# A Strassen-style block product in place of an ordinary one, inside a fused two-layer adapter kernel

## The chip, the core and the metric

The kernel runs on one core of one Trainium2 chip. The metric is the device time of one execution in microseconds, the median of three runs. TensorE (PE) does the matrix products and 128x128 transposes, with weight loads (PEld) that overlap it. VectorE (DVE), ScalarE (ACT) and GpSimd (POOL) work element by element, and SyncE (SP) issues most transfers. The engines run their own programs in order and meet only at semaphores.

## What is computed

The input x is 8 batches of 256 rows by 1024. Two layers are applied, each of which adds to x the result of two adapted linear maps with gates. Cut to the second layer, which the change is about:

```python
base_out = jnp.einsum('bti,oi->bto', x, W) + b          # cond map, 1024x1024
lora_out = jnp.einsum('btr,bro->bto', jnp.einsum('bti,bir->btr', x, A), Bm)   # adapter of the batch
y = base_out + lora_out * SCALING
base = y @ W_base.T + b_base                            # ffn map, 1024x1024
logits = y @ W_router.T                                 # 8 experts, the top 2 are kept
lora = jnp.einsum('ter,te,eor->to', jnp.einsum('td,erd->ter', y, A1), w, B1) * SCALING
x = x + base + lora
```

## The kernel before

Since nothing nonlinear stands between the two maps, the kernel folds them once: M = W · [router, A1, W_base]ᵀ, plus the identity for the residual, is a matrix of 1024 rows (8 tiles of 128) and 1160 columns; 16 more columns hold the adapter A of the batch, so 1176 in all. Each float32 number is split into a high and a low part of the type fp32r, and each product of two split numbers is three matmuls (`three`, L1054 to L1056: hi·hi, hi·lo, lo·hi). The helper `lo` (L705) makes a low part on VectorE, ScalarE copies the high part.

The stages are these. First the weights come in and are turned, and the first layer's small matrices are made (`turn_units`, L1049). Then the **fold** goes over 8 rows of M: each row is 24 steps of `three` in three parts of 392, 512 and 256 columns (`m_chunk`), into one of two sets of three PSUM banks. Beside it VectorE multiplies the bias into `b_acc` (`b_times`, L934), which is written out at the end by six matmuls with `ones`.

Then come eight **slots**, one for each batch, of which the first seven also prepare the next batch. Slots 1 to 4 are a hardware loop. In slot b, TensorE does the **main product** of x1 (the batch after the first layer, turned, hence 8 tiles by 2 halves of 128 rows) with M: 48 steps of `three`, six groups (2 halves by 3 parts of 392 columns) of 8 steps, into the banks `pm`. Among these steps stand, at places written out by hand (`main_to(n)` goes on to step n):

- `small0`: the first layer's 272 columns for one half of the next batch (24 matmuls, L1054 with `C0hi`), twice;
- turns of small gate matrices (`hg`, `wh`, `wz`, L1103, and `hs`, L1244), which VectorE's gate computations `gates0`, `gates1` and `top1` must have made;
- `lora`: for each half 4 matmuls for each of 3 parts (240, 392 and 392 columns), which add the expert part to y;
- `ffn0` in four groups of 6 matmuls of 256 columns: the next batch's first-layer result, which VectorE adds to x (`x1_add`, L871). The groups go to three banks, so that only the fourth waits for an `x1_add`:

```python
                if has_a:
                    pe.wait_ge(whT_lo, a + 2)
                    for g in range(3):
                        ffn0(q, g, X1W_BANKS[g])
                main_to(34)
                turn_hs(m + 1)
                if has_a:
                    pe.wait_ge(x1_sum, q * 4 + 1)
                    ffn0(q, 3, X1W_BANKS[3])
```

The output rows are copied from PSUM to `ybuf` by ScalarE (L572) and stored. GpSimd does nothing in the slots.

## Time and profile before

| what | value |
| --- | --- |
| median of 3 runs | 500.59 us (500.29 to 501.21) |
| the profiled execution | 501.62 us, its span 499.6 us |
| TensorE busy | 487.5 us (98%), 3007 matmuls |
| VectorE, ScalarE, GpSimd busy | 267.6, 135.9 and 9.5 us |
| granted clock of TensorE, mean | 0.989 of 2.4 GHz |

The span goes from the first to the last instruction; about 2 us of the time lie outside it. TensorE is busy almost throughout, and a record of a matmul lasts longer than its share of the array, since matmuls are pipelined: what a matmul costs in a stream is the distance from its start to the next one's start.

### The profile page before, as it was taken

Reading aid. Unit: us, or ns where it says so; the run is one execution under the profiler, and the core shown is the slowest. Engines: PE = TensorE matmul, PEld = TensorE weight load, DVE = VectorE, ACT = ScalarE, POOL = GpSimd, SP = SyncE. Lnnn points to the kernel's source line nnn. Section 1 sums busy time; section 2 is a strip of 40 time slices with the busy share of each in tenths; the row PEclk is TensorE's granted clock in tenths of the full one; section 3 lists DMA queues with packets and bytes.
Section 4 is the critical chain, followed back from the end, with each engine's and each line's share of the span. In section 5 each row is a group of like instructions: output and inputs, shape, how many; then the busy total and the mean of one; then the engine's idle time right before and its main releaser. Section 6 shows DMA issues by size and latency. Waiting matters only on the chain.

```text
span 499.6 us, 8465 instructions
## 1 busy us (share of the span) xinstructions
PE 487.5 (98%) x3007; PEld 466.5 (93%) x3007; DVE 267.6 (54%) x825; ACT 135.9 (27%) x300; POOL 9.5 (2%) x18
## 2 busy tenths in 40 slices
PE   6999999999999988999999999999999999999997
PEld 4988899999999878999999999999999999999997
DVE  3745864544446746475465574656557457445211
ACT  4444630111111331232132232132124123212111
POOL 2040000000000000000000000000000000000000
PEclk9987999999999999999999999999999999999999
DMA  8975525221111145107304312611710910200111
GB/s 258 331 253 178 183 72 139 106 63 43 42 42 48 44 62 78 54 4 120 71 5 95 53 46 64 83 42 60 89 42 2 148 44 2 64 31 16 59 42 43
DMA packets 86621, 40.22 MB, mean 81 GB/s; under 512 B 68503, under 2 KB 80545, under 8 KB 86462
## 3 DMA queue, kind: packets, MB, share of 16 engines
q1 hardware_dynamic: 86318, 39.25, 31.3%
q0 software_dynamic: 272, 0.56, 0.5%
q8 instruction: 19, 0.31, 0.3%
q14 instruction: 12, 0.10, 0.1%
HBM read 28.64 MB, written 11.16 MB: 80 GB/s over the span
## 4 chain that ended last, share of the span: by engine, by line
PE 96%; DVE 2%; DMA 1%; ACT 1%; issue 0%; DVEq 0%; ACTq 0%
PE banks L1054 28%; PE banks L1056 28%; PE banks L1055 28%; PE banks L1049 5%; PE banks L1068 3%; PE banks L1239 2%; PE banks L1103 1%; DMA a0f<-in_L_ffn_A_dram 1%; PE banks L1077 0%; PE banks L1201 0%; PE banks L1244 0%; DVE xTlo L705 0%; DVE x_raw L752 0%; PE banks L1249 0%; DVE a0f L741 0%
## 5 line engine op out<-in xcount | busy, mean ns | idle before, releaser
L1054 PE MATMUL banks<-Mhi,x1Thi 128*128 128x392 f32 x384 | 137.0, 357 | 2.0 <-DVE x1Tlo L705 1.5
L1055 PE MATMUL banks<-Mlo,x1Thi 128*128 128x392 f32 x384 | 130.6, 340 | 0.0
L1056 PE MATMUL banks<-Mhi,x1Tlo 128*128 128x392 f32 x384 | 130.5, 340 | 0.0
L1054 PEld LDWEIGHTS banks<-Mhi,x1Thi 128*128 128x128 f32 x384 | 72.3, 188 | 4.5 <-issue 2.4
L1054 PE MATMUL banks<-WbThi,ws_hi 128*128 128x392 f32 (+2 forms) x216 | 74.7, 346 | 0.0
L1056 PE MATMUL banks<-WbThi,ws_lo 128*128 128x392 f32 (+2 forms) x216 | 73.2, 339 | 0.0
L1055 PE MATMUL banks<-WbTlo,ws_hi 128*128 128x392 f32 (+2 forms) x216 | 73.0, 338 | 0.0
L1055 PEld LDWEIGHTS banks<-Mlo,x1Thi 128*128 128x128 f32 x384 | 72.5, 189 | 0.0
L1056 PEld LDWEIGHTS banks<-Mhi,x1Tlo 128*128 128x128 f32 x384 | 72.2, 188 | 0.0
L1056 PEld LDWEIGHTS banks<-WbThi,ws_lo 128*128 128x128 f32 x216 | 40.7, 188 | 3.2
L1055 PEld LDWEIGHTS banks<-WbTlo,ws_hi 128*128 128x128 f32 x216 | 40.6, 188 | 3.1
L1054 PEld LDWEIGHTS banks<-WbThi,ws_hi 128*128 128x128 f32 x216 | 40.6, 188 | 3.0
L572 ACT ACTIVATE ybuf<-banks 128x392 f32<-128x392 f32 (+1 forms) x48 | 21.8, 454 | 44.3 <-PE banks L1239 44.3
L1054 PE MATMUL banks<-C0hi,xThi 128*128 128x272 f32 x112 | 32.5, 290 | 1.3 <-DVE xTlo L705 1.3
L624 ACT ACTIVATE Mhi<-banks 128x392 f32 (+5 forms) x24 | 10.3, 494 | 81.3 <-DVE banks L951 60.9
L1056 PE MATMUL banks<-C0hi,xTlo 128*128 128x272 f32 x112 | 32.3, 288 | 0.0
L1055 PE MATMUL banks<-C0lo,xThi 128*128 128x272 f32 x112 | 32.2, 287 | 0.0
L503 ACT ACTIVATE x1Thi<-wraw 128x512 fp32r<-128x512 f32 x32 | 19.8, 627 | 21.4 <-DVE wraw L871 19.1
L705 DVE SCALAR_TENSOR_TENSOR Mlo<-banks,Mhi 128x392 f32 (+8 forms) x30 | 15.4, 554 | 16.4 <-ACT Mhi L624 14.4
L1054 PEld LDWEIGHTS banks<-C0hi,xThi 128*128 128x128 f32 x112 | 21.1, 188 | 1.8 <-DVE xTlo L705 1.8
L705 DVE SCALAR_TENSOR_TENSOR x1Tlo<-wraw,x1Thi 128x512 fp32r<-128x512 f32 x32 | 21.1, 682 | 2.2 <-ACT x1Thi L503 2.2
L705 DVE SCALAR_TENSOR_TENSOR xTlo<-x_raw,xThi 128x512 fp32r<-128x512 f32 x28 | 18.1, 688 | 6.9 <-ACT xThi L503 6.9
(180 smaller groups left out, 772.8 us busy)
## 6 DMA issues: line engine op xcount, KB each, us to landing
wraw<-in_L_cond_W_dram SPq DMA_DIRECT2D x16, 512.0 KB, 3.9
out_dram<-ybuf SPq DMA_DIRECT2D x15, 512.0 KB, 3.1
x_raw<-in_x_dram SPq DMA_DIRECT2D x56, 128.0 KB, 3.9
wraw<-in_L_ffn_W_base_dram SPq DMA_DIRECT2D x8, 512.0 KB, 6.5
xin_first<-in_x_dram SPq DMA_DIRECT2D x1, 1024.0 KB, 9.5
x1T_dram<-xin_first SPq DMA_DIRECT2D x1, 1024.0 KB, 3.9
wraw<-x1T_dram SPq DMA_DIRECT2D x2, 512.0 KB, 3.5
Fbuf<-fe_hi_dram SPq DMA_DIRECT2D x16, 64.0 KB
```

Source lines behind the costliest of these rows:

```text
L503: act.activation(dst, src, ACT.Copy).then_inc(ready, 1)
L572: act.activation(ybuf[:, y0:y0 + n], pm[c][:, PART - n:PART], ACT.Copy).then_inc(y_ready, 1)
L624: act.activation(Mhi[:, bass.ds(i * 2 + par, 1), R + c0:R + c0 + n], m_psum(M_BANKS[par], c).unsqueeze(1), ACT.Copy).then_inc(m_hi, 1)
L705: return dve.scalar_tensor_tensor(out=out_, in0=src, scalar=scale, in1=hi.bitcast(F32), op0=ALU.mult, op1=ALU.subtract)
L1049: ins = pe.transpose(unit_bank(q)[:, col:col + width], src, ident[0:kp, 0:kp])
L1054: pe.matmul(out_, l[0], r[0], start=start, stop=False, **kw)
L1055: pe.matmul(out_, l[0], r[1], start=False, stop=False, **kw)
L1056: return pe.matmul(out_, l[1], r[0], start=False, stop=stop, **kw)
L1068: ins = pe.matmul(banks[:, k, 0:2 * RC], w, R0T[:, j, :], start=j == 0 and n == 0, stop=j == K - 1 and n == 1)
L1103: pe.transpose(dst, src, ident[:, :]).then_inc(done, 1)
L1239: pe.matmul(y, hsT[:, :], Fbuf[:, s], start=False, stop=True, skip_group_check=True)\
```

## The change

The main product becomes two parts. 256 of the 1176 columns (16 of the adapter, 136 of router and A1, 104 of y) stay an ordinary product, `zd`: 16 steps of `three`, 256 wide. The other 920 columns are taken as two halves of 460, the 8 tiles of the inner dimension as two groups of 4, and the two row halves as the third split. This 2x2x2 block product is done with seven products (`PRODUCTS`) instead of eight, each of 4 steps of `three` of 460 columns, 28 steps. A slot has 44 steps in place of 48.

The right-hand factors B11, B21, B22 and T1 to T4 are made during the fold (sums of blocks of M, then split into high and low), whose row order becomes 0, 4, 1, 5, ... and whose parts become 240, 460 and 460 columns. The left-hand ones are the blocks A11 to A22 of x1 and the sums S1 to S4, made in place in `x_raw`. GpSimd makes the sums (`s_sums`), the low parts of S3 and S4 (`s_lo_part`) and the low parts of the next x tiles (`xT_lo_part`), which VectorE made before. The products are combined in `ybuf` by six VectorE additions beside copies by ScalarE. The banks are short: all four `ffn0` groups now share the bank `x1w`. The low parts of x1 for a batch are all made before its slot (`a_part`).

```diff
-    MW = MC + R
     ZC = R + RC
-    HALF = D // 2
-
-    PART = MW // 3
-    Y_OF = [(0, PART - ZC), (PART - ZC, PART), (2 * PART - ZC, PART)]
+
+    DW = 256
+    SW = (R + MC - DW) // 2
+    KH = K // 2
+    Y_OF = [(0, DW - ZC), (DW - ZC, SW), (DW - ZC + SW, SW)]
+    CHUNKS = [(0, DW - R), (DW - R, SW), (DW - R + SW, SW)]
     LANG_BIAS = 5.0
...
+            def s_sums(q, turn):
+                raw = x_raw[turn]
+                gp.wait_ge(a_lo, q * 4 + 4)
+                gp.tensor_tensor(raw_block(raw, 1, 1), raw_block(raw, 1, 0), raw_block(raw, 1, 1), ALU.add)\
+                  .then_inc(s_raw, 1)
+                gp.wait_ge(s_raw, q * 4 + 1)
+                sub(raw_block(raw, 1, 0), raw_block(raw, 0, 0), raw_block(raw, 1, 0)).then_inc(s_raw, 1)
+                gp.wait_ge(s12_lo, q * 2 + 1)
+                sub(raw_block(raw, 1, 1), raw_block(raw, 1, 1), raw_block(raw, 0, 0)).then_inc(s_raw, 1)
+                gp.wait_ge(s_raw, q * 4 + 3)
+                sub(raw_block(raw, 0, 1), raw_block(raw, 0, 1), raw_block(raw, 1, 1)).then_inc(s_raw, 1)
+
+            def s_lo_part(q, turn, n):
+                left = left_of(turn)[("S3", "S4")[n]]
+                gp.wait_ge(s_hi, q * 4 + 3 + n)
+                sub(left[:, 1, :], raw_block(x_raw[turn], 1 - n, n), left[:, 0, :].bitcast(F32)).then_inc(s34_lo, 1)
+
+            gp.wait_ge(x_turned, 1)
...
+            def b_times(k):
+
+                for n in range(2):
+                    for c, (c0, w) in enumerate(CHUNKS):
+                        nth = 2 * k + n
+                        dve.wait_ge(acc_step, 3 * nth + c - 1 if nth else 1)
+                        dve.scalar_tensor_tensor(out=b_acc[:, c0:c0 + w], in0=Wb_of[c][n][:, k, :].bitcast(F32),
+                                                 scalar=bcol[:, k:k + 1], in1=b_acc[:, c0:c0 + w],
+                                                 op0=ALU.mult, op1=ALU.add).then_inc(acc_step, 1)
...
+                par, row, p = s % 2, M_ROWS[s], s // 2
+                add_ident(s)
+                dve.wait_ge(w1_hi, s + 3)
+                lo(ws_lo[par][:, :], wraw[2 + par][:, :], ws_hi[par][:, :]).then_inc(w1_lo, 1)
+                dve.wait_ge(m_hi, m_hi_at(s, 1))
+                lo(direct(1, row), m_psum(par, 0), direct(0, row)).then_inc(m_lo, 1)
+                if p < 2 and par == 0:
+                    dve.wait_ge(m_hi, m_hi_at(s, 2))
+                    lo_right(p, B11, m_psum(par, 1), m_lo)
+                    dve.wait_ge(m_hi, m_hi_at(s, 3))
+                    sub(right_raw(p, T1), right_raw(p, T3), m_psum(par, 1), m_lo)
+                elif p < 2:
+                    dve.wait_ge(m_hi, m_hi_at(s, 3))
+                    sub(right_raw(p, T3), m_psum(par, 2), right_raw(p, T3), m_lo)
+                    sub(right_raw(p, T2), m_psum(par, 2), right_raw(p, T1), m_lo)
+                    lo_right(p, B21, m_psum(par, 1))
+                    lo_right(p, B22, m_psum(par, 2))
...
+                for k in ((s,), (4, 5), (6, 7))[max(0, s - 3)]:
+                    b_times(k)
+            dve.wait_ge(x2_in, 128)
+            for half in range(2):
+                turn_x(half, x_raw[1])
+
+            for s in (LAST, K - 1):
+                dve.wait_ge(m_hi, m_hi_at(s, 1))
+                lo(direct(1, M_ROWS[s]), m_psum(s % 2, 0), direct(0, M_ROWS[s])).then_inc(m_lo, 1)
...
+                s_part(b, turn, 1)
                 if has_a:
                     gates0(a, q)
+                hs_part(m, 0)
+                if has_a:
                     hgT_part(a)
-                hs_part(m)
+                hs_part(m + 1, 1)
                 if has_a:
                     top1(a)
-                    if first:
-                        turn_x(1, x_raw[1], x_in[1], 64)
-                        xT_turned(a + 1, 1, x_raw[1])
-                    gates1(m, lambda: whT_part(a, 0))
-                    gates0(a + 1, q, lambda: wzT_part(m))
-                    if has_n:
-                        turn_x(0, x_raw[turn], x_in[0], b * 64 + 64)
+                gates1(m, 0, (lambda: whT_part(a, 0)) if has_a else None)
+                gates1(m + 1, 1, None)
+                wzT_part(m)
+                if has_a:
+                    gates0(a + 1, q)
+                keep_p16(b)
+                if has_a:
                     hgT_part(a + 1)
+                if has_n:
+                    dve.wait_ge(x_in[0], b * 64 + 64)
+                    turn_x(0, x_raw[turn])
+                keep_p15(b)
+                if has_a:
                     top1(a + 1)
+                wzT_part(m + 1)
+                if has_a:
                     whT_part(a + 1, 1)
-                    if has_n:
-                        xT_turned(n, 0, x_raw[turn])
-                    add(0)
-                    hs_part(m + 1)
-                    add(1)
-                    split(0)
-                    add(2)
-                    gates1(m + 1, lambda: add(3))
-                    split(1)
-                    wzT_part(m + 1)
-                    split(2)
-                    split(3)
-                else:
-                    gates1(m, None)
-                    wzT_part(m)
-                    hs_part(m + 1)
-                    gates1(m + 1, None)
-                    wzT_part(m + 1)
                 if has_n:
-                    turn_x(1, x_raw[turn], x_in[1], b * 64 + 128)
-                    xT_turned(n + 1, 1, x_raw[turn])
+                    dve.wait_ge(x_in[1], b * 64 + 64)
+                    turn_x(1, x_raw[turn])
+                if has_a:
+                    x1_add(q, 0, raw)
+                    x1_add(q, 1, raw)
+                    x1_add(q, 2, raw)
+                    a_part(q, 1 - turn, 0)
+                keep_p167(b)
+                if has_a:
+                    x1_add(q, 3, raw)
+                    a_part(q, 1 - turn, 1)
+                    a_part(q, 1 - turn, 2)
+                    a_part(q, 1 - turn, 3)
+                y_c21(b)
+                y_c22(b)
                 if has_a:
                     as_part(q)
-            slot(0, 0, True, True, first=True)
+                    s_part(q, 1 - turn, 0)
+                y_c12(b)
...
             turn_units(NU2, units_b1)
-            pe.wait_ge(w1_lo, K)
-            pe.wait_ge(m_lo, 3 * (K - 2))
-            m_chunk(K // 2 - 1, 1, 0)
+            pe.wait_ge(m_kept, 2)
+            m_chunk(0, 1)
+            pe.wait_ge(acc_step, 1 + 6 * K)
+            pe.wait_ge(gp_step, 3)
+            pe.wait_ge(m_lo, m_lo_at(K - 1, 1))
+
+            def bias_part(c):
+                c0, n, _ = BIAS_PARTS[c]
+                pe.matmul(bias_psum(c), ones[:, :], b_acc[:, c0:c0 + n], start=True, stop=True).then_inc(bias_done, 1)
+
+            bias_part(0)
+            bias_part(1)
+            pe.wait_ge(m_kept, 4)
+            m_chunk(1, 1)
+            pe.wait_ge(brow_lo, 1)
+            bias_part(2)
+            m_chunk(0, 2)
+            m_chunk(1, 2)
...
+                PRODUCTS = [("A11", B11, ca, True), ("S2", T2, cb, True), ("A22", T4, ce, True), ("S1", T1, cd, True),
+                            ("A12", B21, ca, False), ("S3", T3, cb, False), ("S4", B22, cd, False)]
...
                     turn_small(wh_ready, a + 2, pt_wh, wh[:, :], twh_done)
-                main_to(31)
+                main_to(38)
                 if has_a:
                     pe.wait_ge(whT_lo, a + 2)
-                    for g in range(3):
-                        ffn0(q, g, X1W_BANKS[g])
-                main_to(34)
-                turn_hs(m + 1)
-                if has_a:
-                    pe.wait_ge(x1_sum, q * 4 + 1)
-                    ffn0(q, 3, X1W_BANKS[3])
-                main_to(35)
-                adapter(m + 1)
-                main_to(44 if has_n else 46)
-                turn_small(wz_ready, m + 2, pt_wz, wz[:, :], twz_done)
-                main_to(47 if has_n else 48)
-                pe.wait_ge(wzT_lo, m + 2)
-                lora(m + 1, 0)
-                lora(m + 1, 1)
-                main_to(48)
-                lora(m + 1, 2)
+                    pe.wait_ge(y_act, b * 3 + 1)
+                    for g in range(4):
+                        if g:
+                            pe.wait_ge(x1_sum, q * 4 + g)
+                        ffn0(q, g, x1w)
+                        main_to(39 + g)
+                main_to(42)
+                lora(m + 1, 1, 0)
+                lora(m + 1, 1, 1)
+                main_to(43)
+                pe.wait_ge(c_kept, b * 3 + 3)
+                lora(m + 1, 1, 2)
+                main_to(44)
```

The order of instructions shows three places. The first is TensorE in slot 0, between two groups of `ffn0` for the next batch (`whThi,BwThi` is the first matmul of three). Before:

```order
L1054 MATMUL banks<-whThi,BwThi 128x256
L1055 MATMUL banks<-whTlo,BwThi 128x256
L1056 MATMUL banks<-whThi,BwTlo 128x256
L1054 MATMUL banks<-whThi,BwThi 128x256
L1055 MATMUL banks<-whTlo,BwThi 128x256
L1056 MATMUL banks<-whThi,BwTlo 128x256
```

After the change, the same place (`G,left` is a step of a Strassen product, 460 wide):

```order
L1350 MATMUL banks<-whThi,BwThi 128x256
L1351 MATMUL banks<-whTlo,BwThi 128x256
L1352 MATMUL banks<-whThi,BwTlo 128x256
L1350 MATMUL banks<-G,left 128x460
L1351 MATMUL banks<-G,left 128x460
L1352 MATMUL banks<-G,left 128x460
L1350 MATMUL banks<-whThi,BwThi 128x256 [waits x1_sum]
L1351 MATMUL banks<-whTlo,BwThi 128x256
L1352 MATMUL banks<-whThi,BwTlo 128x256
```

Between two groups stands one product step now, and the next group has a wait for `x1_sum`, the addition of the group ahead of it.

The second is VectorE from the end of slot 0 over the branch into the loop. Before:

```order
L705 SCALAR_TENSOR_TENSOR wzTlo<-banks,wzThi 128x128 [waits wzT_hi]
L705 SCALAR_TENSOR_TENSOR x1Tlo<-wraw,x1Thi 128x512 [waits x1T_hi] x2
L752 STREAM_TRANSPOSE x_raw<-x_raw 128x1024 [waits x_in1]
L705 SCALAR_TENSOR_TENSOR xTlo<-x_raw,xThi 128x4x128 [waits xT_hi] x2
L705 SCALAR_TENSOR_TENSOR Mlo<-asraw,Mhi 128x8x16 [waits as_hi]
L1031 UNCONDITIONAL_BRANCH
L1031 ISA
L779 ISA [waits p0_done]
```

After, where `left<-x_raw,left` is the low part of S1 in the first row and of S2 in the fifth:

```order
L909 SCALAR_TENSOR_TENSOR left<-x_raw,left 128x512 [waits s_hi]
L1084 TENSOR_TENSOR ybuf<-banks,ybuf 128x460 [waits p_done]
L1327 UNCONDITIONAL_BRANCH
L1327 ISA
L909 SCALAR_TENSOR_TENSOR left<-x_raw,left 128x512 [waits s_hi]
L977 ISA
L978 ISA [waits p0_done]
L978 TENSOR_TENSOR lgc<-banks,bias 128x8
```

The gates of the new slot (`lgc`, which waits for `p0_done`) now stand behind the low part of S2 and no more right behind the adapter's split.

The third is GpSimd's program at the end of the fold. Before, its last instructions:

```order
L481 TENSOR_TENSOR C0lo<-a0f,C0hi 128x4x136 [waits c0_hi]
L481 TENSOR_TENSOR C0lo<-b_j,C0hi 128x4x136 [waits c0_hi]
L484 DMA a0c<-in_L_ffn_A_dram 128x1024 [waits unit_done]
L485 DMA routers<-in_L_ffn_W_router_dram 8x1024
L488 COPY b_j<-b0raw 128x1024 [waits b1_in,c0_lo]
L490 MEMSET Fbuf 96x1024 [waits m_done]
```

After, `x_raw<-x_raw` are the four sums of `s_sums(0, 0)`:

```order
L596 TENSOR_TENSOR x_raw<-x_raw 128x512 [waits a_lo]
L586 TENSOR_TENSOR x_raw<-x_raw 128x512 [waits s_raw]
L586 TENSOR_TENSOR x_raw<-x_raw 128x512 [waits s12_lo]
L586 TENSOR_TENSOR x_raw<-x_raw 128x512 [waits s_raw]
L586 TENSOR_TENSOR xTlo<-x_raw,xThi 128x512 [waits xT_hi] x2
L586 TENSOR_TENSOR left<-x_raw,left 128x512 [waits s_hi] x2
```

The third sum, the one for S2, waits for `s12_lo`, the low part of S1 on VectorE, since it overwrites S1.

## Rows read from the trace of the kernel before

**Rows 1.** The page, busy time of each engine and the chain that ended last.

```profile
PE 487.5 (98%) x3007; PEld 466.5 (93%) x3007; DVE 267.6 (54%) x825; ACT 135.9 (27%) x300; POOL 9.5 (2%) x18
...
PE 96%; DVE 2%; DMA 1%; ACT 1%; issue 0%; DVEq 0%; ACTq 0%
```

**Rows 2.** The chain of waits, TensorE alone: waited for, us in total, times, longest.

```profile
PE banks L1054 <- DVE x1Tlo L705: 1.5, 1, 1.5
PE banks L1054 <- DVE xTlo L705: 1.3, 1, 1.3
```

**Rows 3.** Windows, one steady slot and the last slot.

```profile
231.54:271.63 40.09, 40.09 (x258) 39.73 (x257) 23.06 (x87) 10.71 (x27) 0.00 (x0) 1.00 0.36 62
466.10:499.60 33.50, 30.48 (x174) 29.76 (x174) 5.28 (x30) 4.52 (x13) 0.00 (x0) 0.98 0.15 54
```

**Rows 4.** Timeline of TensorE from a slot's start: start us, us, instruction.

```profile
224.82 0.29 PE L1054 MATMUL banks<-C0hi,xThi 128*128 128x272 f32 x1
...
227.81 0.34 PE L1054 MATMUL banks<-Mhi,x1Thi 128*128 128x392 f32 x1
...
231.54 0.27 PE L1103 MATMUL banks<-ident,hg 128*128 128x128 f32 x1
```

**Rows 5.** Timeline of TensorE: 240 columns, and 136 columns.

```profile
29.32 0.28 PE L1056 MATMUL banks<-R0T,b0lo 128*128 128x136 f32 x1
29.43 0.28 PE L1054 MATMUL banks<-R0T,b0hi 128*128 128x136 f32 x1
...
302.58 0.27 PE L1054 MATMUL banks<-ws_hi,wzThi 128*128 128x240 f32 x1
...
303.03 0.34 PE L1054 MATMUL banks<-ws_hi,wzThi 128*128 128x392 f32 x1
```

**Rows 6.** Timeline of TensorE: the parts of one fold row, and what follows.

```profile
152.54 0.34 PE L1054 MATMUL banks<-WbThi,ws_hi 128*128 128x392 f32 x1
...
156.84 0.39 PE L1054 MATMUL banks<-WbThi,ws_hi 128*128 128x512 f32 x1
...
162.41 0.28 PE L1054 MATMUL banks<-WbThi,ws_hi 128*128 128x256 f32 x1
...
165.24 0.27 PE L1049 MATMUL banks<-ident,wraw 128*128 128x128 f32 x1
```

**Rows 7.** Groups by line and form: busy us, mean ns, idle before.

```profile
L871 DVE TENSOR_TENSOR wraw<-banks,x_raw 128x512 f32<-128x512 f32 x28 | 19.2, 687 | 1.2 <-PE banks L1056 1.1
L705 DVE SCALAR_TENSOR_TENSOR x1Tlo<-wraw,x1Thi 128x512 fp32r<-128x512 f32 x32 | 21.1, 682 | 2.2 <-ACT x1Thi L503 2.2
L705 DVE SCALAR_TENSOR_TENSOR Mlo<-banks,Mhi 128x392 f32 x6 | 3.4, 567 | 8.9 <-ACT Mhi L624 8.9
L934 DVE SCALAR_TENSOR_TENSOR b_acc<-WbTlo,bcol,b_acc 128x1160 f32<-128x1160 f32 x8 | 11.4, 1427 | 0.9
L752 DVE STREAM_TRANSPOSE x_raw<-x_raw 128x1024 f32<-128x1024 f32 x14 | 17.3, 1236 | 0.0
L503 ACT ACTIVATE x1Thi<-wraw 128x512 fp32r<-128x512 f32 x32 | 19.8, 627 | 21.4 <-DVE wraw L871 19.1 <-PE banks L1056 2.2
L481 POOL TENSOR_TENSOR C0lo<-a0f,C0hi 128x544 fp32r<-128x544 f32 x1 | 1.4, 1353 | 0.4 <-ACT C0hi L525 0.4
```

**Rows 8.** Timeline of all engines: the gates of a slot, and the turned gate.

```profile
228.13 0.17 DVE L779 TENSOR_TENSOR lgc<-banks,bias 128x8 f32<-128x8 f32 x1 [0.76 <-PE banks L1056]
...
230.20 0.29 DVE L774 TENSOR_TENSOR hg<-banks,gc 128x128 f32<-128x128 f32 x1
...
231.91 0.28 ACT L503 ACTIVATE hgThi<-banks 128x128 fp32r<-128x128 f32 x1 [3.01 <-PE banks L1103]
232.22 0.29 DVE L705 SCALAR_TENSOR_TENSOR hgTlo<-banks,hgThi 128x128 fp32r<-128x128 f32 x1 [1.73 <-ACT hgThi L503]
```

**Rows 9.** Timeline: TensorE goes on after a wait for VectorE.

```profile
222.82 0.38 PE L1054 MATMUL banks<-ws_hi,wzThi 128*128 128x240 f32 x1 [0.21 <-DVE wzTlo L705]
223.03 0.28 PE L1055 MATMUL banks<-ws_lo,wzThi 128*128 128x240 f32 x1
```

More of the change, by code:

```diff
@@ L493, in _ @@
+            slot(0, 0, True, True)
+            with gp.Fori(0, 2) as i:
+                for turn in (1, 0):
+                    slot(i * 2 + 2 - turn, turn, True, True)
+            slot(NB - 3, 1, True, True)
+            slot(NB - 2, 0, True, False)
+            slot(NB - 1, 1, False, False)
         @block.scalar
@@ L650, in _ @@
-            keep_m(K // 2 - 1, 1, (2,))
-            def slot(b, turn, has_a, has_n, first=False):
+                    a_part(0, 0, 0)
+                act.wait_ge(bias_done, c + 1)
+                keep(b_acc[0:64, c0:c0 + n].bitcast(F32R), bias_psum(c)[0:64, :], brow_hi)
+            act.wait_ge(m_done, m_count(K - 1, 1))
+            for which, i in ((B11, 0), (B21, 2), (B22, 3)):
+                keep(right(2, which)[0], m_raw[:, i, :], g2_hi)
+            act.wait_ge(m_ident, LAST + 1)
+            keep(right(3, B11)[0], m_psum(0, 1), g3_hi)
@@ L865, in x1_first, with x1_add @@
                    .then_inc(x1_sum, 1)
[L867 removed]
+            def x1_add(q, g, raw):
                 dve.wait_ge(x1w_done, q * 4 + g + 1)
[L870 to L875 removed]
@@ new lines, in main_to @@
+                def main_to(until):
+                    for step in range(done[0], until):
+                        if step < 2 * K:
+                            half, k = step // K, step % K
+                            name = ("A11", "A12", "A21", "A22")[step // KH]
+                            if step == 0:
+                                pe.wait_ge(a_lo, b * 4 + (2 if first else 3))
+                                if first:
+                                    pe.wait_ge(m_lo, m_lo_at(K - 1, 1))
+                            if step == K:
+                                wait_earlier(pe, y_act, b * 3 if not first else 0)
+                                pe.wait_ge(a_lo, b * 4 + 4)
+                                if first:
+                                    pe.wait_ge(g3_lo, 2)
+                            ins = three(zd[half][:, :], (rows(left[name][:, 0, :], k % KH), rows(left[name][:, 1, :], k % KH)),
+                                        (Mdir[:, 0, k, :], Mdir[:, 1, k, :]), k == 0, k == K - 1, skip_group_check=True)
+                            if k == K - 1:
+                                ins.then_inc(h1_done, 1)
+                        else:
+                            i, k = steps[step - 2 * K]
+                            name, which, bank, fresh = PRODUCTS[i]
+                            if k == 0:
+                                before(i)
+                            if first and step == 2 * K:
+                                pe.wait_ge(g_lo, 8)
+                                pe.wait_ge(g2_lo, 7)
+                            if first and k == KH - 1:
+                                pe.wait_ge(g3_lo, 7 if i else 1)
+                            ins = three(bank, (rows(left[name][:, 0, :], k), rows(left[name][:, 1, :], k)),
+                                        right(k, which), fresh and k == 0, k == KH - 1, skip_group_check=True)
+                            if k == KH - 1:
+                                ins.then_inc(p_done, 1)
```

775 lines of the change are left out of this document (479 added, 296 removed).

## The prediction

> **What bounds the kernel now.** First the page: TensorE is busy for 487.5 of the span's 499.6 us, it has 96% of the chain that ended last, and VectorE, at 267.6, has 2% of it [rows 1]. So what counts is the length of TensorE's stream and its holes. Then TensorE's waits: inside the work only two are over 1 us, 1.5 and 1.3, both for low parts by VectorE at the passage from the fold to slot 0 [rows 2]. Then the windows: a steady slot is 40.1 us without a hole, at clock 1.00; VectorE is busy for 23.1 of it, ScalarE for 10.7, GpSimd not at all. The last slot is 33.5, 30.5 of it TensorE [rows 3]. Last the timeline, for what a matmul costs from start to start (start times below are differences of its rows). 21 matmuls of 392 columns take 3.73 us, .178 each, and 24 of 272 take 2.99, .125 [rows 4]. A fold row of 24 each of 392, 512 and 256 takes 4.30, 5.57 and 2.83: .179, .232 and .118 [rows 6]. The cost isn't in proportion to the columns: four of 240 take .45, .1125 each, and one of 136 takes .11 as well [rows 5]. Below 240 columns nothing more is saved. For 460 I lay a line between 392 and 512: .178 + 68/120 x .053 = **.208**.
>
> **The change part by part.** The sum is made against the profiled execution, 501.62.
>
> *Main product.* Before, 144 matmuls at .178 = 25.6 us in a slot. After, 16 x 3 at .118 and 28 x 3 at .208 = 5.7 + 17.5 = 23.1. 8 batches by 2.5: **-20.0**. If .208 is wrong by .005, this moves by 3.4.
>
> *Adapter output (`lora`).* Its parts go from 240, 392, 392 to 104, 460, 460. A set of one each: .1125 + 2 x .178 = .47, and .11 + .416 = .53. Four matmuls of each part, two halves, eight batches: 64 x .057 = **+3.7**. If a 104-wide matmul cost in proportion (.05) it would be 0; the 136-wide row is the nearest, so I take the floor.
>
> *Fold parts.* 24 x (.1125 + .416) = 12.7, as before (12.70): **0**.
>
> *The one bank of `ffn0`.* A group may start only when `x1_add` has emptied the bank. Group: 6 x .118 = .71, of which the last record ends .16 after the next could start (.28 against .118) [rows 6], so .87. The hop to VectorE .1 (ScalarE starts on the turned gate at 231.91, .1 after the record that began at 231.54 ended [rows 4, 8]); `x1_add` .69 [rows 7]; hop back .1; and the stream takes .1 more to fill (.21 instead of .11 after a wait [rows 9]). That is 1.8 us from group to group. In it lie the group and one step of a product, .71 + 3 x .208 = 1.33. The hole is .45, three times in seven slots: **+9.5**. Here VectorE has nothing else in its way, since the first three additions follow each other; the fourth has a low part and a copy ahead of it, which I take to fit in. Lower bound: if the end of the record is not what VectorE waits for, .2 to .3 a hole, 4 to 6 in all.
>
> *Slot 0.* Behind the fold's last matmul VectorE has the identity .3, ten operations of 460 columns at .6 (blocks of M, from the 392-wide .57), the low part of S1 .68: 7.3. GpSimd's third sum waits for that one: 1353 ns for 544 columns [rows 7] is 1.27 for 512, so 8.6. ScalarE .63, low part of S2 .68: 9.95. Behind it stand the gates, 2.35 from `lgc` to the end of `hg` (228.13 to 230.49) [rows 8]: 12.3. TensorE is at the turn of `hg` after 24 matmuls of the adapter, 3.0, and 12 steps of 3 x .118, at 7.3. It waits **+5.0**; `small0` and the product would be its cover, and both stand ahead. Bounds: 3, if half the VectorE operations lie before the fold's end, and 7.
>
> *End of the fold.* From the end of the sixth row VectorE has identity, `ws_lo` and a direct block, 3.3; the bias sweeps of two rows, four of them, 1.43 each as one piece [rows 7] and some 1.65 cut in three: 10.0; two transposes of 1.24: 12.5; two direct low parts: 13.2. TensorE has two 240-wide parts, a turn and one 460-wide part ahead of the bias matmuls, 2 x 2.7 + .8 + 5.0 = 11.2. **+2.0** (0 to 4). It is queued behind `acc_step` and the last `m_lo` alike.
>
> *Small terms.* The turning stage, where some units are split: **+.5** (0 to 2). The waits of [rows 2] go, since the blocks of A are ready before the slot: **-2.8**. The tail has two 460-wide additions at .63 one after the other instead of one copy: **+.3**.
>
> *In the steady slots*, the chain of S sums decides whether the gates hold TensorE up. From the slot's start: last low part of A at -1.0; first sum .35; high part 1.05, low part 1.75; third sum 3.05; high 3.75, low part of S2 4.45; gates 6.85. TensorE needs `hg` at 7.3. The slack is .4, so nothing is added. The other gate turns have .15 to .6 by the same count. VectorE's load goes from 23 to about 25.5 of 39, ScalarE's to about 12.5, GpSimd's from 0 to ten operations, 12.7. These are far from full. Slots of about 39.4.
>
> Sum: -20.0 + 3.7 + 9.5 + 5.0 + 2.0 + .5 - 2.8 + .3 = **-1.8**. So 499.8 against 501.62; the median of before is 500.59, 1.0 lower, and so is the forecast: **498.8**.
>
> **The rivals.**
>
> *The holes are half of what I walked.* A walk by mean durations adds each hop in full. If the ring costs .2 (-5), slot 0 and the fold's end 3.5 in place of 7 (-3.5) and `lora` nothing for its narrow part (-3.5 at most), the sum is about -12: **488.6**. For it: the kernel before shows hardly any wait but in [rows 2], with queues as long. Against: 136 columns at the price of 240 [rows 5], and a bank that is one instead of three. Chance .30.
>
> *GpSimd and VectorE hold each other up.* All ten GpSimd operations of a slot read two SBUF operands, while VectorE makes low parts of S and A from two SBUF operands too, and parts of the gates. No row of before has both at once: GpSimd's 1353 ns operation ran beside VectorE work with at most one SBUF operand, and the slots had no GpSimd work. If an operation of the one waits for the end of the other, each meeting costs up to 1.27 on VectorE's side or .68 on GpSimd's. The chain of S has two or three such places and a slack of .4, so 1.5 to 2.5 us of each of six slots would be lost, and 2 more in slot 0: +11 to +17, **about 511**. It decides from .5 us a slot on. For it: 12.7 us of GpSimd beside 25.5 of VectorE in 39. Against: no row. Chance .24. This is the case in which the kernel is slower.
>
> The Trainium skill, page "SBUF — State Buffer", section "Who interferes with whom", says that a VectorE instruction with two SBUF inputs contends with a GpSimd instruction that reads SBUF, and that the second then waits until the first has ended. By that rule this rival is the forecast; no trace here shows it so far.
>
> *A GpSimd sum takes longer than its only row*, by half, or the chain has more hops: 1.5 us late against a slack of .4 to .5 gives +1.0 in seven slots: **505.5**. Chance .12.
>
> **How the numbers follow.** The forecast as walked, within 3 us: .34, of which .19 lie on the faster side, .08 within and .07 on the slower. ±.2%, 1 us, is about what a measurement of this kernel can tell from no change. The half-size holes: .30 faster. The two slower rivals: .36, of which .02 within. That is .49 faster, .10 same, .41 slower. The predicted time is the forecast's, 498.8, which also lies between the cases; its own range is 495.5 to 502. The range for 8 in 10 reaches to both sides: 487 (the small holes, with 1.5 of room) to 511 (the lock).
>
> **What would show it.** Right: 460-wide matmuls .208 apart, 104-wide ones .11; waits for `x1_sum` of .4 to .5, three in a slot; one of about 5 us at the first turn of `hg` in slot 0 and of about 2 ahead of the bias matmuls; steady slots of 39.4 without a wait for gates; the last slot's TensorE time down from 30.5 to about 28.5 (-2.5 + .5). Wrong: GpSimd operations over 1.4 us or VectorE's low parts over .75 whenever both run (the lock); the `x1_sum` waits at .2 (the small holes); or waits for `hg`, `wz` or S high parts in every slot, which would say that my slack of .4 was none.

## The result: 526.5 us in place of 500.8, five per cent slower

The changed kernel takes 526.47 us (median of 4 runs, 525.70 to 527.38), the kernel before 500.80 on the same chip: a ratio of 1.049 (1.045 to 1.054). The forecast was 498.8, with a range up to 511. One execution of the kernel before, of 2687 us, counts as slow and is in none of the ratios below.

The page of the changed kernel, busy time of each engine and the chain that ended last, beside [rows 1]:

```profile
PE 483.9 (92%) x2911; PEld 438.3 (84%) x2911; DVE 341.3 (65%) x923; ACT 154.1 (29%) x339; POOL 112.0 (21%) x98
...
PE 48%; issue 24%; DVE 13%; POOL 8%; ACT 3%; DMA 2%; SPq 0%; POOLq 0%; DVEq 0%; ACTq 0%
```

TensorE has less work than before, and it isn't the bound any more: VectorE and GpSimd together have 21% of the chain. VectorE's busy time grew by 74 us. The forecast gave it 2.5 us more a slot; a good part of the rest isn't work but operations that last longer, as is seen below.

TensorE's waits (waited for, us in total, times, longest), beside [rows 2]:

```profile
PE banks L1399 <- DVE hg L973: 23.0, 7, 7.5
...
PE banks L1350 <- DVE x_raw L1069: 2.2, 14, 0.2
```

`hg` is the gated adapter tile of the next batch's first half. It is waited for once in each of the seven slots that prepare a batch. The second row is the one bank of `ffn0`.

Windows by stage, slot 0, slots 1 to 5, slot 6 and the last one. First the kernel before (length, then busy time of PE, PEld, DVE, ACT and POOL, clock, DMA share, GB/s):

```profile
184.15:224.82 40.67, 39.17 (x249) 38.16 (x248) 25.09 (x91) 10.41 (x27) 0.00 (x0) 1.00 0.35 54
224.82:425.37 200.55, 200.55 (x1282) 198.82 (x1281) 115.46 (x437) 54.18 (x137) 0.00 (x0) 1.00 0.32 60
425.37:465.60 40.23, 40.23 (x257) 39.61 (x256) 19.38 (x83) 9.25 (x25) 0.00 (x0) 1.00 0.11 34
465.60:499.60 34.00, 30.54 (x175) 29.80 (x174) 5.57 (x31) 4.99 (x14) 0.00 (x0) 0.98 0.15 53
```

The same stages of the changed kernel:

```profile
183.05:232.68 49.63, 41.65 (x244) 38.02 (x245) 34.93 (x102) 14.92 (x36) 14.50 (x12) 0.90 0.20 28
232.68:447.76 215.08, 199.78 (x1221) 181.62 (x1220) 151.49 (x456) 58.41 (x145) 63.87 (x51) 0.98 0.31 56
447.76:490.35 42.59, 39.26 (x246) 35.29 (x244) 26.59 (x91) 10.64 (x28) 10.71 (x10) 1.00 0.11 33
490.35:523.90 33.55, 28.37 (x162) 25.74 (x162) 12.16 (x39) 5.51 (x14) 6.33 (x5) 0.96 0.18 69
```

The differences: up to slot 0 -1.1 us, slot 0 +9.0, slots 1 to 5 +14.5, slot 6 +2.4, the last slot -.5. Together 24.3, the whole growth of the span (499.6 to 523.9). So the loss is not in the fold but in every slot that has gates for a next batch.

What ends late is seen in slot 2 of the changed kernel. VectorE from the low part of S1 to `hg` (start us, us, instruction, idle before it and what ended that):

```profile
275.75 1.22 DVE L909 SCALAR_TENSOR_TENSOR left<-x_raw,left 128x512 fp32r<-128x512 f32 x1 [0.54 <-ACT left L656]
...
279.03 1.23 DVE L909 SCALAR_TENSOR_TENSOR left<-x_raw,left 128x512 fp32r<-128x512 f32 x1 [1.51 <-ACT left L656]
280.18 0.15 DVE L978 TENSOR_TENSOR lgc<-banks,bias 128x8 f32<-128x8 f32 x1
...
281.51 1.33 DVE L1003 TENSOR_SCALAR gac<-iota,ixfc,wc 128x8 f32<-128x8 f32 x1
282.76 1.30 DVE L1006 TENSOR_SCALAR gbc<-iota,ixfc,wc 128x8 f32<-128x8 f32 x1
284.10 0.17 DVE L1009 TENSOR_TENSOR gc<-gac,gbc 128x8 f32<-128x8 f32 x1
284.63 0.29 DVE L973 TENSOR_TENSOR hg<-banks,gc 128x128 f32<-128x128 f32 x1 [0.37 <-DVE gc L1009]
```

And GpSimd in the same stretch:

```profile
275.13 1.29 POOL L586 TENSOR_TENSOR x_raw<-x_raw 128x512 f32<-128x512 f32 x1
277.05 2.66 POOL L586 TENSOR_TENSOR x_raw<-x_raw 128x512 f32<-128x512 f32 x2 [0.63 <-DVE left L909]
281.54 2.50 POOL L586 TENSOR_TENSOR xTlo<-x_raw,xThi 128x512 fp32r<-128x512 f32 x2 [1.83 <-ACT xThi L656]
```

Lay the two beside each other. The low part of S1 starts at 275.75, while GpSimd's sum runs until 276.42, and it ends .55 after that: 1.22 us for an operation of .68. So an operation of VectorE seems to wait here until one of GpSimd has ended; the expectations below call this the lock theory. `gac` and `gbc` have 8 elements a lane; each reads one tile and two scalars per lane. They take 1.3 us each, as long as each of GpSimd's two low parts of x, with which they start and end. Before, with GpSimd idle, they were these:

```profile
229.49 0.28 DVE L804 TENSOR_SCALAR gac<-iota,ixfc,wc 128x8 f32<-128x8 f32 x1
229.68 0.28 DVE L807 TENSOR_SCALAR gbc<-iota,ixfc,wc 128x8 f32<-128x8 f32 x1
```

From `lgc` to the end of `hg` it was 2.36 us [rows 8]; now it is 4.74. `hg` is there 10.1 us after the slot's start (274.81), the forecast had 6.85.

TensorE behind it:

```profile
281.92 0.28 PE L1352 MATMUL banks<-Mdir,left 128*128 128x256 f32 x1
284.98 0.33 PE L1399 MATMUL banks<-ident,hg 128*128 128x128 f32 x1 [2.79 <-DVE hg L973]
...
286.00 0.42 PE L1350 MATMUL banks<-Mdir,left 128*128 128x256 f32 x1
286.22 0.42 PE L1351 MATMUL banks<-Mdir,left 128*128 128x256 f32 x1
286.43 0.41 PE L1352 MATMUL banks<-Mdir,left 128*128 128x256 f32 x1
```

It waits 2.79 us, and some .8 us after it goes on, matmuls of 256 columns stand .21 apart instead of .12. That is the second price of the wait, the clock:

```profile
282.10:285.00 2.90, 0.11 (x2) 0.02 (x2) 2.50 (x5) 0.00 (x0) 1.93 (x2) 1.00 0.00 0
285.00:287.00 2.00, 2.00 (x13) 2.00 (x13) 0.49 (x3) 0.28 (x1) 0.00 (x0) 0.67 0.01 4
287.00:288.00 1.00, 1.00 (x7) 1.00 (x6) 0.00 (x0) 0.00 (x0) 0.00 (x0) 0.50 0.00 0
...
291.00:300.00 9.00, 9.00 (x56) 8.39 (x56) 6.02 (x37) 2.29 (x7) 1.31 (x1) 1.00 0.48 70
```

The granted clock (the column after the five engines) is at .50, that is 1.2 GHz, for about 3 us. By the starts this costs 1.4 us here: the first 60 matmuls behind the wait take 10.1 us, and 8.7 in the slots in which the clock stays up. It happens in three of the six later slots, and in slot 0 it costs 2.4 us by the same count: 6.6 us in all.

### The profile page after: what moved, and what is told of

Same layout as the page of the kernel before. It is cut to its first block, busy times and chain, and to the rows that moved or that the text cites. A ratio compares the mean times of both kernels' runs of the same rounds, so it can differ in the third digit from the quotient of the medians.

```text
span 523.9 us, 8531 instructions
## 1 busy us (share of the span) xinstructions
PE 483.9 (92%) x2911; PEld 438.3 (84%) x2911; DVE 341.3 (65%) x923; ACT 154.1 (29%) x339; POOL 112.0 (21%) x98
## 4 chain that ended last, share of the span: by engine, by line
PE 48%; issue 24%; DVE 13%; POOL 8%; ACT 3%; DMA 2%; SPq 0%; POOLq 0%; DVEq 0%; ACTq 0%
PE banks L1350 13%; PE banks L1352 13%; PE banks L1351 13%; PE banks L1364 3%; PE banks L1345 3%; POOL x_raw L586 3%; DVE left L909 2%; POOL xTlo L586 2%; POOL left L586 2%; DVE G L909 2%; POOL x_raw L596 1%; ACT left L656 1%; DVE gbc L1006 1%; DVE b_acc L1181 1%; DVE x_raw L1069 1%
## 5 line engine op out<-in xcount | busy, mean ns | idle before, releaser
L1350 PE MATMUL banks<-G,left 128*128 128x460 f32 x224 | 89.9, 401 | 0.0
L1351 PE MATMUL banks<-G,left 128*128 128x460 f32 x224 | 84.5, 377 | 0.0
L1352 PE MATMUL banks<-G,left 128*128 128x460 f32 x224 | 83.8, 374 | 0.0
L586 POOL TENSOR_TENSOR xTlo<-x_raw,xThi 128x512 fp32r<-128x512 f32 x28 | 35.2, 1278 | 193.6 <-ACT xThi L656 193.6
L1350 PE MATMUL banks<-WbThi,ws_hi 128*128 128x460 f32 (+1 forms) x216 | 75.2, 348 | 0.5 <-DVE Mdir L909 0.5
L1352 PE MATMUL banks<-WbThi,ws_lo 128*128 128x460 f32 (+1 forms) x216 | 73.4, 340 | 0.0
L1351 PE MATMUL banks<-WbTlo,ws_hi 128*128 128x460 f32 (+1 forms) x216 | 73.1, 338 | 0.0
L656 ACT ACTIVATE left<-x_raw 128x512 fp32r<-128x512 f32 x64 | 38.7, 627 | 82.8 <-DVE x_raw L1069 28.9
L909 DVE SCALAR_TENSOR_TENSOR left<-x_raw,left 128x512 fp32r<-128x512 f32 x48 | 39.4, 835 | 18.3 <-ACT left L656 17.8
L1350 PEld LDWEIGHTS banks<-G,left 128*128 128x128 f32 x224 | 43.4, 194 | 5.1 <-DVE wzTlo L909 0.2
L1352 PEld LDWEIGHTS banks<-G,left 128*128 128x128 f32 x224 | 43.1, 192 | 4.8
L1351 PEld LDWEIGHTS banks<-G,left 128*128 128x128 f32 x224 | 43.4, 194 | 2.6
L1350 PEld LDWEIGHTS banks<-WbThi,ws_hi 128*128 128x128 f32 x216 | 40.6, 188 | 3.7 <-DVE ws_lo L909 0.6
L1352 PEld LDWEIGHTS banks<-WbThi,ws_lo 128*128 128x128 f32 x216 | 40.7, 188 | 3.0
L1350 PE MATMUL banks<-Mdir,left 128*128 128x256 f32 x128 | 38.1, 298 | 0.3 <-DVE Mdir L909 0.3
L1352 PE MATMUL banks<-Mdir,left 128*128 128x256 f32 x128 | 37.1, 290 | 0.0
L1351 PE MATMUL banks<-Mdir,left 128*128 128x256 f32 x128 | 37.1, 290 | 0.0
L586 POOL TENSOR_TENSOR x_raw<-x_raw 128x512 f32<-128x512 f32 x24 | 31.0, 1290 | 9.4 <-DVE left L909 8.2
```

Source lines behind the costliest of these rows:

```text
L586: return gp.tensor_tensor(out_, a, b, ALU.subtract)
L656: act.activation(dst, src, ACT.Copy).then_inc(ready, 1)
L909: return dve.scalar_tensor_tensor(out=out_, in0=src, scalar=scale, in1=hi.bitcast(F32), op0=ALU.mult, op1=ALU.subtract)
L1350: pe.matmul(out_, l[0], r[0], start=start, stop=False, **kw)
L1351: pe.matmul(out_, l[0], r[1], start=False, stop=False, **kw)
L1352: return pe.matmul(out_, l[1], r[0], start=False, stop=stop, **kw)
```

## The experiments

Times before slot 0 vary by 3 us between profiles of these kernels (slot 0 starts at 182.1 to 185.4). Nearly all of that lies ahead of the fold, whose first matmul starts at 48.8 to 51.6, while weights come in and are turned; from there to slot 0 it is 133.3 to 134.0 us in every profile. So each is judged by its slots too, and not by its total alone.

### The wait for GpSimd, taken apart

**late_xt.** GpSimd makes the two low parts of x later:

```diff
                 if has_a:
+                    gp.wait_ge(hg_ready, a + 1)
                     xT_lo_part(a + 1, 1, x_raw[1 - turn])
```

> The changed kernel with one wait more: GpSimd makes the low parts of the next x tile (xTlo) only after the first gate of the slot (hg) is ready. Lock theory: in the changed kernel the two 8-element operations gac and gbc last 1.3 us each beside GpSimd instead of .28, and with .2 more they are the last 2.2 us ahead of hg. They fall back to .28, the wait of TensorE for hg falls from 2.5 to 2.8 us a slot to about .5 (7.5 to about 5.3 in slot 0), and the stretch of half clock behind it (1.5 us in some slots) goes too: about 526.5 - 7 x 2.2 - 4 = 507. Rival (the walk was too short, or GpSimd's operations are simply long, and VectorE's own queue sets the time): hg comes at the same time, 526.

Measured: 507.25 us, ratio 1.0122 (1.0101 to 1.0144). One more wait makes the kernel 19 us faster. The chain of waits and the window of slots 1 to 5:

```profile
PE banks L1400 <- DVE hg L974: 8.6, 7, 5.5
```

```profile
231.00:431.64 200.64, 195.64 (x1222) 177.36 (x1220) 141.51 (x456) 58.41 (x145) 64.16 (x51) 1.00 0.32 60
```

`gac` and `gbc` are at 284 ns on average, the waits for `hg` at .4 to .7 in slots 1 to 6, slots 1 to 5 take 200.6 us instead of 215.1, and the clock there is 1.00. The rival, a long queue, falls: nothing was taken out of VectorE's queue.

**clear.** The sums for S3 and S4 go behind `hg` too:

```diff
+            def s_late(q, turn):
+                raw = x_raw[turn]
+                gp.wait_ge(s_raw, q * 4 + 2)
+                sub(raw_block(raw, 1, 0), raw_block(raw, 0, 0), raw_block(raw, 1, 0)).then_inc(s_raw, 1)
+                sub(raw_block(raw, 0, 1), raw_block(raw, 0, 1), raw_block(raw, 1, 1)).then_inc(s_raw, 1)
...
+                    gp.wait_ge(hg_ready, a + 1)
                     xT_lo_part(a + 1, 1, x_raw[1 - turn])
+                s_late(b, turn)
                 s_lo_part(b, turn, 0)
```

> As the one before, and the sums for S3 and S4 on GpSimd move behind hg as well (GpSimd then makes only the sums for S1 and S2 before it). Lock theory: the low parts of S1 and S2 fall from 1.2 to .68 us each, the third sum starts .65 earlier, hg is ready about 6.9 us after the slot's start, as the prediction walked it, and TensorE does not wait for it in steady slots; in slot 0 about 4 us stay. Steady slots of 40.1 (38.4 of stream, 1.3 of the x1_sum holes); about 503. Rival (the chain is long by its hops): a wait of 1.5 to 2 us stays in every slot, about 515.

Measured: 510.45, ratio 1.0186 (1.0164 to 1.0208), 7 us over what was expected. The part about the lock came true (no wait for `hg` in slots 1 to 6). But the chain of waits has a new row:

```profile
PE banks L1605 <- ACT hsT L661: 7.2, 6, 1.4
PE banks L1404 <- DVE hg L978: 5.0, 1, 5.0
```

ScalarE stood waiting for the late sum of S3, and the copy of `hsT`, which was ready, stood behind it in its queue.

**clear2.** Only ScalarE's order changes:

```diff
-                s_part(b, turn, 2)
                 hsT_part(m, 0)
                 hsT_part(m + 1, 1)
                 if has_a:
                     whT_part(a, 0)
                 exp1(m)
+                s_part(b, turn, 2)
                 keep_p1(b)
```

> The kernel clear, with ScalarE's high part of S3 behind its two copies of hsT and its exponential of the second gates (in clear, ScalarE stood waiting for the late sum of S3 with hsT queued behind it, and TensorE waited 1.2 us for hsT in each of six slots). If that queue was the only new cost of clear, the hsT waits go, steady slots are 39.4, and the time is 510.5 - 7.2 = 503.3. Rival (the late sums for S3 and S4 hold up VectorE's top-1 operations, which they now meet, and so something else): slots stay at 40.5 and the time at 509 to 510.

Measured: 506.14 (503.13 to 508.02), ratio 1.0093 (1.0060 to 1.0126). The waits for `hsT` are gone, and one for `wh` is there, 2.9 us in six slots, so that the time is between the two theories. This run shows the gates of slot 2 with GpSimd out of the way, VectorE:

```profile
269.15 0.69 DVE L914 SCALAR_TENSOR_TENSOR left<-x_raw,left 128x512 fp32r<-128x512 f32 x1 [0.54 <-ACT left L661]
269.76 0.63 DVE L1089 TENSOR_TENSOR ybuf<-banks,ybuf 128x460 f32<-128x460 f32 x1
272.05 0.69 DVE L914 SCALAR_TENSOR_TENSOR left<-x_raw,left 128x512 fp32r<-128x512 f32 x1 [1.66 <-ACT left L661]
...
274.00 0.28 DVE L1008 TENSOR_SCALAR gac<-iota,ixfc,wc 128x8 f32<-128x8 f32 x1
274.19 0.28 DVE L1011 TENSOR_SCALAR gbc<-iota,ixfc,wc 128x8 f32<-128x8 f32 x1
...
275.05 0.29 DVE L978 TENSOR_TENSOR hg<-banks,gc 128x128 f32<-128x128 f32 x1 [0.37 <-DVE gc L1014]
```

The slot starts at 268.21. The low part of S2 ends 4.5 us later (the walk in the prediction: 4.45), `hg` 7.1 us later (6.85), and TensorE turns it at 275.44 without a wait. The addition into `ybuf`, which has one input from PSUM, takes its .63 although GpSimd starts a sum at 270.00, in its midst. So an operation of this kind is not held up.

**clear3.** GpSimd's late sums wait for `wh` as well:

```diff
+                if has_a:
+                    gp.wait_ge(wh_ready, a + 1)
                 s_late(b, turn)
```

> clear2, with GpSimd's late sums for S3 and S4 held back until wh is ready: in clear2 the first of them held up the top-1 operations (ixft .49, gt 1.20 us), and TensorE waited .5 us for wh in each of six slots. Lock theory: gt falls to .29, the wh waits go, steady slots of 39.4 to 39.6, 3 us less than clear2 where the time before slot 0 is the same. Rival: S3 is late now and the slots stay at 39.7 to 40.1.

Measured: 506.66 (506.03 to 507.34), ratio 1.0113 (1.0082 to 1.0144), no better than clear2. Slots are 39.8 to 40.1, in clear2 39.7 to 40.5. The waits for `wh` are gone, and the second turn of `hg` has one of .38 in six slots instead: the second layer's gate operations `gaf` and `gbf`, .28 each when alone, are at .81 on average (.69 and .74 in clear2), and what follows them is late. GpSimd's work is 12.8 us of a slot, and in each of the four places tried it meets some gate. A kernel that gives the sums back to VectorE or ScalarE was not run.

### The same in the kernel before

**bef_gp_read** and **bef_gp_write** add GpSimd operations on tiles of their own to the kernel before, with nothing of the block product. The core of the first (the second has two `memset` of 128x1024 behind a tiny addition):

```diff
+                    gp.wait_ge(g0_step, a * 8 + 4)
+                    gp.tensor_tensor(gp_out[:, :], gp_in[:, :], gp_in[:, :], ALU.add).then_inc(gp_extra, 1)
+                    gp.wait_ge(gp_extra, b * 2 + 2)
+                    gp.tensor_tensor(gp_out[:, :], gp_in[:, :], gp_in[:, :], ALU.add).then_inc(gp_extra, 1)
```

> The kernel before, with nothing of the block product, and two extra GpSimd additions of 128x512 from SBUF to SBUF on tiles of their own in each of the first seven slots, started when the reciprocal of the first gate is done. Lock theory: gac and gbc take up to 1.3 us each in these seven places, hg comes 1.5 to 2 us later, which is .5 to 1 us more than its slack of 1.0, and each slot grows by .5 to 1: 504 to 507. Rival (the stretch needs the block product's own loads on the engines): both stay at .28 and the time at 500.6.

> As the one before, but the two GpSimd operations are fills of 128x1024, which read nothing (started by a tiny addition of 8 columns). If the operations gac and gbc are held up only by GpSimd's reads, they stay at .28 and the time at 500.6. If any GpSimd access to SBUF holds them up, they take .6 to 1 us, and the time goes to 501 to 504.

Measured: 504.61, ratio 1.0075 (1.0049 to 1.0101), with additions, and 506.36, ratio 1.0100 (1.0077 to 1.0123), with fills. Slots grow from 40.1 to 40.6 and 40.7, some 3.5 and 4 us over seven slots; the rest of the second run's growth lies ahead of slot 0. One slot with additions:

```profile
229.94 1.04 POOL L500 TENSOR_TENSOR gp_out<-gp_in 128x512 f32<-128x512 f32 x1 [38.86 <-DVE wc L820]
229.97 1.04 DVE L823 TENSOR_SCALAR gac<-iota,ixfc,wc 128x8 f32<-128x8 f32 x1
...
230.92 0.28 DVE L826 TENSOR_SCALAR gbc<-iota,ixfc,wc 128x8 f32<-128x8 f32 x1
231.06 1.04 POOL L502 TENSOR_TENSOR gp_out<-gp_in 128x512 f32<-128x512 f32 x1
231.24 0.89 DVE L829 TENSOR_TENSOR gc<-gac,gbc 128x8 f32<-128x8 f32 x1
```

One with fills:

```profile
231.21 1.98 DVE L823 TENSOR_SCALAR gac<-iota,ixfc,wc 128x8 f32<-128x8 f32 x1
231.31 0.95 POOL L502 MEMSET gp_out<- 128x1024 f32 x1
231.40 1.79 DVE L826 TENSOR_SCALAR gbc<-iota,ixfc,wc 128x8 f32<-128x8 f32 x1
...
232.20 0.96 POOL L503 MEMSET gp_out<- 128x1024 f32 x1
...
233.24 0.17 DVE L829 TENSOR_TENSOR gc<-gac,gbc 128x8 f32<-128x8 f32 x1
```

`gac`, with 8 elements a lane, ends .03 us behind GpSimd's first 512-column addition, and `gc` .03 behind the second. The rival, that the stretch needs the block product's load, falls. `gac`, which reads one tile and two scalars per lane, is held up by both kinds, and through both fills, though its record starts .10 us before the first of them, beside the tiny addition; that only GpSimd's reads would do it is refuted for this operation. `gc`, an addition of two tiles in SBUF, is held up by GpSimd's additions (.89). With fills it starts only when they have ended, so what a fill does to such an operation isn't shown.

The Trainium skill, page "SBUF — State Buffer", section "Who interferes with whom", makes this distinction: two SBUF inputs contend with GpSimd's reads only, while `copy`, `cast` and `tensor_scalar` can run in modes that use both of VectorE's port pairs and then contend with any GpSimd access. The traces agree for `gac` and `gbc`, beside reads and fills, and for the cast `ixft` beside reads, which takes up to .87 instead of .17 in the changed kernel.

### The other terms

**ring2** (on clear2) and **ring3** (on clear3) put a second product step into two of the three `ffn0` holes (groups at steps 36, 38, 40, 41 of 44). Turns, VectorE's additions and GpSimd's low parts of x move to suit. The core of it, in ring3:

```diff
                 main_to(36)
...
-                main_to(38)
...
-                        main_to(39 + g)
+                        main_to((38, 40, 41, 42)[g])
```

> clear2, with two product steps instead of one between the first, second and third groups of ffn0 (groups at steps 36, 38, 40 and 41 of 44 instead of 38, 39, 40, 41; the turns of wz and wh ahead of them move up, one transpose of x on VectorE moves behind the first addition, and GpSimd's low parts of x for the next slot wait for wh). If each hole is .42 us (1.77 from group to group against 1.35 of stream): two of three holes go, 14 x .42 = 5.9 less than clear2. Rival (the holes only move, since whT or the additions are late then): within 1.5 us of clear2.

Measured for ring2: 508.73 (506.89 to 509.48), ratio 1.0142 (1.0114 to 1.0171), not better than clear2. Two holes went, and TensorE waits for `wzTlo` instead, .7 in each of seven slots: ScalarE may overwrite `wzThi` only when the adapter part has read it, and `wh` stood behind. ring3 turns `wh` first:

> clear3, and the ffn0 groups at steps 36, 38, 40 and 41 as in ring2. There the holes of two groups went (.84 us a slot), but the wait for wzTlo took their place: ScalarE may write wzThi only when the adapter part of the first half has read it, so the turn of wz could not move up, and wh stood behind it in the same bank. Now wh is turned first and wz one step later. If that was all: no wait for wzTlo, slots .84 shorter than in clear3, 38.6 to 38.8, and 5.9 us less than clear3. Rival (a new wait for whTlo or for x1_sum): 0 to 2 us less.

Measured for ring3: 501.99, ratio 1.0015 (.9997 to 1.0033). That is 4.7 us under clear3, of which 1.1 lies ahead of the fold in the profiles; slots are 39.3 to 39.8 instead of 39.8 to 40.1, some .44 less each. In clear3 it is 1.66, 1.76 and 1.76 us from group to group, and a group with one step is 1.34 of stream (6 x .118 + 3 x .21), so the holes are .32, .42 and .42. In ring3 the first two are gone (1.95 and 1.97, with two steps between), and the turn of `wz` has a wait of .28 in their place: .46 by this count. So the holes were real, and close to the .45 that was walked.

**tail2** stores the last rows in four pieces:

```diff
+                sp.wait_ge(y_act, b * 3 + 3)
+                sp.wait_ge(y_dve, b * 3 + 1)
+                early = Y_OF[2][0]
+                sp.dma_start(rows_of[1][:, 0:early], ybuf[1][:, 0:early]).then_inc(y_out[1], 16)
...
                 sp.wait_ge(y_dve, b * 3 + 2)
-                sp.dma_start(rows_of[1], ybuf[1][:, :]).then_inc(y_out[1], 16)
+                sp.dma_start(rows_of[1][:, early:D], ybuf[1][:, early:D]).then_inc(y_out[1], 16)
```

> clear2, but the last batch's rows are stored in four pieces, each as soon as its additions are done, where the second tile's 512 KB went out in one piece behind its last addition. In the changed kernel the time from TensorE's last instruction to the end grew from 3.0 to 5.2 us. If the size of that last store is the cause: 1.5 us less than clear2. If it is the two additions in a row (1.27 us), about 0.3 less.

Measured: 504.62 (503.59 to 504.96), ratio 1.0064 (1.0044 to 1.0085), 1.5 under clear2, whose times (503.13 to 508.02) reach below and above it. The profiles decide: from the end of TensorE's last matmul to the end of the span it is 4.1 us instead of 5.4, a gain of 1.3, where the two additions in a row would have given .3. So the size of the last store was the larger part of the growth from 3.0 us.

**slot0** puts the gates of slot 0 ahead of the last low parts on VectorE:

```diff
+            gates0(2, 1)
+            s_part(0, 0, 0)
+            hgT_part(2)
+            hs_part(0, 0)
+            t_lows(((0, T1), (1, T3)))
+            hs_part(1, 1)
+            s_part(0, 0, 1)
+            t_lows(((2, T2), (3, T4)))
```

> clear2, with slot 0 in another order on VectorE and ScalarE: the gates for the next batch ahead of the last four low parts of T, of S1 and of S2, which the products need later. TensorE waits 5.0 us for hg there in clear and runs at half clock for some 3 us behind the wait (1.5 us more). If the order of VectorE's queue is the cause: 5 to 6.5 us less than clear2. Rival (the same work is only late somewhere else, at S2): 0 to 3 us less.

Measured: 506.62 (506.01 to 507.16), ratio 1.0107 (1.0088 to 1.0126): no gain. The wait for `hg` went (5.0 to 0), and 4.5 us for `wh` came. Slot 0 is 46.3 instead of 46.5. Here both engines hold each other up, GpSimd:

```profile
192.86 3.31 POOL L586 TENSOR_TENSOR xTlo<-x_raw,xThi 128x512 fp32r<-128x512 f32 x2
196.13 3.33 POOL L586 TENSOR_TENSOR x_raw<-x_raw 128x512 f32<-128x512 f32 x2
```

and VectorE:

```profile
192.57 2.47 DVE L919 SCALAR_TENSOR_TENSOR G<-G_raw,G 128x460 fp32r<-128x460 f32 x2
...
195.26 1.46 DVE L919 SCALAR_TENSOR_TENSOR left<-x_raw,left 128x512 fp32r<-128x512 f32 x1
196.64 1.70 DVE L919 SCALAR_TENSOR_TENSOR G<-G_raw,G 128x460 fp32r<-128x460 f32 x1
```

Two operations of GpSimd take 3.3 us instead of 2.5, the low parts of T 1.2 to 1.7 instead of .63.

**all2** joins ring3, tail2 and a better order of slot 0 (the top-1 operations ahead too, the four low parts of T behind the second gates):

> ring3, with the last stores in four pieces as in tail2 (1.3 us less), and in slot 0 the gates and the top-1 operations ahead of the low parts of S2 and T; the four low parts of T come only behind the second gates, since their products are late in the slot. In the run slot0 the wait for hg (5.0 us) went, and one for wh (4.5) came, since top-1 stood behind the low parts of T, which took up to 1.66 us each beside GpSimd. If the queue's order is the cause, slot 0 loses 4 to 6 us: 5 to 7 us less than ring3, about 491 to 493, ahead of the kernel before. Rival (VectorE simply has too much work there): slot 0 as long as in ring3, 1.3 us less.

Measured: 498.71 (497.22 to 501.50), ratio .9949 (.9922 to .9977), faster than the kernel before, by half a per cent. Slot 0 is 42.5 instead of 46.5. It is 3.3 us under ring3, where 5 to 7 were expected. In the profiles slot 0 gives 4.0 and the end .9, and 2.7 are lost ahead of slot 0, whose start is at 185.2 here and at 182.5 in ring3. All of that lies ahead of the fold (first matmul at 51.6 against 48.9), where the change touches nothing. In slot 0 a wait of 1.1 us for a low part of T and one of 1.5 for the second `hg` remain.

## Why the prediction was wrong

**What failed** is the step "The slack is .4, so nothing is added", for the steady slots. Each link of the chain was priced by a row in which the engine was alone. That pricing was right where they are alone (clear2: 4.5 and 7.1 us against 4.45 and 6.85 walked). With GpSimd beside it the chain is 3.1 us longer: .54 for the low part of S1, .54 for that of S2, 2.06 for `gac` and `gbc`. The .4 of slack is set against it, and 2.45 to 2.79 of wait come out.

**The rival was right.** "GpSimd and VectorE hold each other up" had a chance of .24, with 1.5 to 2.5 us a slot. The mechanism and almost the size were there. Missing from it was the place with the largest price, two operations with one tile input, and what a wait costs beyond itself: 6.6 us at 1.2 GHz. So even its 511 was too low (its own terms, +11 to +17 on the forecast, give 510 to 516).

**Slot 0.** +5.0 forecast for the wait, 7.5 measured. In clear, with GpSimd's low parts of x out of the way, it is 4.96: again the walk, without GpSimd beside it. The agreement is in part luck, since the terms of its first sum (.3, ten times .6, .68) make 7.0 and not the 7.3 that it went on with; VectorE really ended the low part of S1 7.4 us into the slot.

**The rest, by terms.** Main product -20.0 forecast: in the last slot, where no gates for a next batch disturb, TensorE is busy for 28.4 us instead of 30.5, -2.2 with the adapter's +.5 in it: -2.6 or -2.7 a slot, close to the 2.5 forecast. Starts of 460-wide matmuls are .214 apart on average there, of 392-wide ones .182; both are a little over the rates taken, since a product's first matmul costs .08 more. `lora` +3.7: a set of three parts goes from .47 to .53 a matmul, +3.9 in all, right; a 104-wide one is mostly .11 from the next. The bank of `ffn0` +9.5: 1.66, 1.76 and 1.76 from group to group (1.8 walked, though the walk's terms add up to 1.86), 8.1 in all, close. End of the fold +2.0: .5 of wait at the bias matmuls, and from the fold's first matmul to slot 0 it is 133.3 us instead of 133.8, so too much. The tail +.3: from TensorE's end to the span's end it is 5.2 instead of 3.0; the two additions were counted, the last store behind them was not. In the rival of the small holes the sum was off as well: its terms at full size make -13.8, not about -12.

Put together, in the profiled executions: the span grew by 24.3 where -1.8 was forecast, a miss of 26.1. About 18 us of `hg` waits beyond the forecast (23.0 against 5.0), 6.6 of half clock and 1.9 of tail make 26.5. That these nearly fill it is in part luck: the fold and the holes came out lower than forecast, and the slots somewhat longer (slots 1 and 4 without their waits: 39.6, where 39.4 was forecast).

## What to carry to other kernels

Before work is given to an idle GpSimd, list which VectorE operations will run beside it, and take each that reads two tiles in SBUF, and each cast or `tensor_scalar` from SBUF to SBUF with more than one element a lane, at up to the length of the GpSimd operation beside it, or of two that follow each other at once (a copy from SBUF to SBUF beside GpSimd is in none of the traces); if such ones sit in a chain with less slack than that, GpSimd's work needs a wait that keeps it out, as in late_xt, where one line gave back 19 us. A slack worked out from durations of engines that ran alone is only good for a schedule in which they do. And a block product that saves 2.6 us of matmuls in 40 pays only if every stage around it keeps up: here it took an order of its own for four engines to get .5%.
